# A graph network on one core: the row-index lookups of the second layer move from the relation loop to ahead of the second message stage

## The chip, the cores and the metric

The kernel runs on one core of a Trainium2 chip. The metric is the device time of one execution in microseconds (us), lower is better. Engines are named as in the profile: PE is TensorE (its weight loads stand apart as PEld), DVE is VectorE, ACT is ScalarE, POOL is GpSimd, and SP is SyncE, which here only issues DMAs.

## The reference

Four graph layers on 625 nodes of 768 features and 10,000 edges, each behind a layer norm with relu and added to `x`. What matters here is the first two. Layer L0 is two relational convolutions in a row with 8 relations, layer L1 is one with 34 relations, followed by a graph convolution:

```python
def _rgcn_conv(x, src, dst, etype, W, root, b):        # L0, twice, 8 relations
    seg = dst * num_rel + etype
    sums = segment_sum(x[src], seg); cnt = segment_sum(ones, seg)
    mean = (sums / maximum(cnt, 1)).reshape(num_nodes, num_rel, -1)
    return einsum('nri,rio->no', mean, W) + x @ root + b

# L1: the same with 34 relations, then xw = h1 @ W_gcn and a
# degree-normed sum over the edges
# L2: two attention layers (8 heads, then 1); L3: one with 12 heads
```

## The kernel before

**Tiles.** The nodes are NG = 5 groups of 128. The edges are sorted by destination group in the kernel and stand in NT = 84 tiles of 128 edges. The sum over edges is not taken first, as in the reference, but last: for each relation r the kernel computes `h @ W[r]` for the nodes and stores the rows to an array `U` in HBM; then, edge tile by edge tile, it gathers the 128 rows of `U` that the edges need and adds them to their destinations with a matmul against a weighted one-hot.

**Stages, in the order of the engines' own programs.** Phase C1 (products of the first convolution, 8 relations), messages 0; phase C2 (second convolution), messages 1; layer norm; the relation stage of L1 (34 relations in 17 pairs), messages 2; then the graph convolution and the attention layers. A product step is 18 matmuls of 128x384 (weights and activations are split into a high and a low part, `w_hi`, `w_lo`, `hT_hi`, `hT_lo`; ACT copies the high part, DVE subtracts for the low part, "the split", L848 and L1040). SP loads the weight halves into two buffers `raw` and stores the results.

**Message stages.** `gathers(phase)` on POOL (L472 to L479) issues 84 indirect DMAs from `U`, 384 KB each, into a ring of RB = 8 buffers; before each it waits until PE is done with the tile that had the buffer (`agg_pe`). PE (`messages`, L1471) waits for the one-hot of DVE (L965) and for the gather. The index table of phases 0 and 1 is `ix[:, 0]`; that of phase 2 is `ix[:, 3]`.

**Why L1 needs a lookup.** In L1 most nodes are no source of a given relation, so the products run on compact lists: for each relation the kernel lists its source nodes (at most TC x 128 = 256 in the main part, the rest in "further" tiles), gathers only these rows of `h` and multiplies them. Where the row of node n in relation r stands in `U` is then no longer r x 640 + n; it is in a table `urow`, which DVE computes in `sources` (L968) in phase C2 and signals with `key_ok`. SP stores it to `urow_d` in HBM inside phase C2 (L327 to L330, `urow_st`). POOL looks up, for each of the 84 edge tiles, 128 words of `urow_d` by the indices `ix[:, 1]` (an indirect DMA into one column of `urow_g`) and casts six columns at a time to integers in `ix[:, 3]` (`urow_out`, L505 to L508).

**POOL's program around the change.** The queue is in order. (1) The kinv loop, L483 to L489: 7 rounds of GU = 12 indirect DMAs in two groups of GB = 6, each group behind an index copy (`indices`, L466). (2) `gathers(0)`. (3) Wait for `ov_ok`, which DVE gives in `further_list` (L988 to L1000) after the last relation of phase C2: a scan, two operations of 6,528 elements on one partition (L991, L994) and a few small ones. Then the waits for the stores of C2 and `gathers(1)`. (4) The relation stage: an unrolled list of 17 blocks b. In each, for two relations, POOL waits until PE has turned the old rows (`hc_tp`), and gathers TC = 2 x 128 rows of `h_d` with indices straight from `lidx`. In blocks 0 to 13 six lookups follow, and in 1 to 14 the cast of the block before. (5) The further tiles and `gathers(2)`.

**Beside POOL in phase C2.** After `sources`, DVE transposes the keys (`keys`) and then writes, between the splits, the one-hots of the 34 node lists (`list_one_hot`, L1002, five f16 operations each), with which PE makes `lidx` (L1112).

**The relation stage on the other engines.** PE does per pair 8 product steps, 24 transposes of gathered rows (L1588) and, in pairs 0 to 13, six tiles of edge counts for the graph convolution (L1468), whose one-hots DVE writes two tiles ahead (L918, L954). ACT waits for the weight half (L607) and for PE, copies it, evacuates the products.

## Time and profile before

| | us |
|---|---|
| time, median of 3 runs | 2400.8 (2396.45 to 2413.4) |
| profiled run: device time | 2400.8 |
| profiled run: span of the trace | 2399.0 |
| PE busy | 2065.2 (86%) |
| DVE busy | 1118.9 (47%) |
| ACT busy | 722.4 (30%) |
| POOL busy | 556.2 (23%) |
| DMA, all queues | 378.31 MB, mean 158 GB/s |

All positions in time are microseconds from the start of the span of the profiled run. The busy time of PE is modelled at its ends, since matmuls overlap. "idle before, releaser" is how long the engine stood before an instruction and whose work ended that wait. A row of the order of time reads: start, duration, engine, line of the kernel, operation, what is written from what.

### The profile page before, as it was taken

To read this page: it belongs to the slowest core of one execution; us is meant where nothing else is said; L and a number is where in the kernel's file an instruction comes from. 1 tells how busy PE (TensorE), PEld (TensorE's weight loads), DVE (VectorE), ACT (ScalarE), POOL (GpSimd) and SP (SyncE) were. 2 spreads that over 40 slices of the span, in tenths; PEclk is the share of its full clock that TensorE was granted. 3 is DMA by queue.
4 is the path that set the end of the run, shared out by engine and by line. 5 is a ranking of instruction groups with operands and counts; after the bars stand their busy time and mean duration, and the time that the engine had idled before them with its cause. 6 is when DMAs were issued, how large, how long until landed. Compare 5 with 4: busy or idle time off the path is not lost.

```text
span 2399.0 us, 33918 instructions
## 1 busy us (share of the span) xinstructions
PE 2065.2 (86%) x10740; PEld 1728.6 (72%) x10741; DVE 1118.9 (47%) x2046; ACT 722.4 (30%) x944; POOL 556.2 (23%) x538
## 2 busy tenths in 40 slices
PE   3999789989999999689999999967989768767885
PEld 3999787558789985389989999964556746647663
DVE  5752122234343652435555555532233776656773
ACT  1222121012212210035545554531010256312763
POOL 0000765630000046324444453104620000000000
PEclk8999899999999999889999999988999889885998
DMA  3556456844446458548878777857840021110111
GB/s 108 156 157 185 137 152 210 267 151 130 138 148 188 154 175 268 173 130 264 262 255 261 251 259 250 267 194 238 268 156 8 0 68 28 53 31 26 53 50 38
DMA packets 203264, 378.31 MB, mean 158 GB/s; under 512 B 18810, under 2 KB 173626, under 8 KB 203176
## 3 DMA queue, kind: packets, MB, share of 16 engines
q1 hardware_dynamic: 170520, 246.23, 31.7%
q0 software_dynamic: 31216, 128.89, 17.6%
q10 hardware_dynamic: 1440, 1.97, 0.2%
q8 instruction: 62, 1.02, 0.2%
q14 instruction: 26, 0.21, 0.0%
HBM read 288.68 MB, written 88.34 MB: 157 GB/s over the span
## 4 chain that ended last, share of the span: by engine, by line
PE 74%; DVE 10%; issue 6%; DMA 4%; ACT 4%; ACTq 0%; another core or an unknown queue 0%; SPq 0%; DVEq 0%; POOL 0%; POOLq 0%
PE ps L1575 41%; PE ps L1483 14%; PE ps L1773 5%; PE ps L1738 2%; DMA arena<-in_L_gnn_W_rel 2%; PE ps L1588 2%; PE ps L1701 1%; PE ps L1809 1%; ACT arena L731 1%; PE ps L1468 1%; PE ps L1466 1%; PE ps L1824 1%; PE ps L1427 1%; DVE counts L899 1%; DVE arena L1240 1%
## 5 line engine op out<-in xcount | busy, mean ns | idle before, releaser
L1575 PE MATMUL ps<-w_hi,hT_hi 128*128 128x384 f32 x2172 | 766.0, 353 | 62.3 <-issue 25.6
L1575 PE MATMUL ps<-w_hi,hT_lo 128*128 128x384 f32 x2172 | 738.5, 340 | 0.8 <-issue 0.8
L1575 PE MATMUL ps<-w_lo,hT_hi 128*128 128x384 f32 x2172 | 738.3, 340 | 0.0
L1575 PEld LDWEIGHTS ps<-w_hi,hT_hi 128*128 128x128 f32 x2172 | 418.1, 193 | 75.0 <-issue 54.4
L1575 PEld LDWEIGHTS ps<-w_lo,hT_hi 128*128 128x128 f32 x2172 | 418.2, 193 | 0.2
L1575 PEld LDWEIGHTS ps<-w_hi,hT_lo 128*128 128x128 f32 x2172 | 416.7, 192 | 1.0 <-issue 0.9
L478 POOL DMA_INDIRECT arena<-U,ix x252 | 252.6, 1002 | 521.5 <-DVE ov L1000 355.0
L1483 PE MATMUL ps<-arena,onehot 128*128 128x512 f32 x1008 | 336.6, 493 | 32.2 <-issue 19.7
L1483 PEld LDWEIGHTS ps<-arena,onehot 128*128 128x128 f32 x1008 | 189.8, 191 | 179.6 <-issue 167.7
L1040 DVE TENSOR_TENSOR w_lo<-arena,w_hi 128x2304 fp32r<-128x2304 f32 x67 | 171.4, 2558 | 139.0 <-ACT w_hi L609 131.3
L558 ACT ACTIVATE arena<-ps 128x384 f32<-128x384 f32 x160 | 78.3, 491 | 494.5 <-PE ps L1575 449.1
L965 DVE TENSOR_SCALAR onehot<-iota,tab,wgt 128x128 f32<-128x128 f32 x252 | 82.2, 360 | 270.6 <-PE ps L1483 236.5
L848 DVE TENSOR_TENSOR w_lo<-arena,w_hi 128x2304 fp32r<-128x2304 f32 x45 | 114.9, 2555 | 165.4 <-ACT w_hi L551 134.2
L514 POOL DMA_INDIRECT h<-h_d,lidx x68 | 100.6, 1480 | 317.1 <-PE ps L1588 272.6
L609 ACT ACTIVATE w_hi<-arena 128x2304 fp32r<-128x2304 f32 x67 | 142.5, 2127 | 54.7 <-DMA arena<-in_L_gnn_W_rel 48.3
L1773 PE MATMUL ps<-arena,R 128*65 128x320 f32 (+1 forms) x400 | 125.4, 437 | 30.6 <-ACT arena L731 30.5
L614 ACT ACTIVATE arena<-ps 128x384 f32<-128x384 f32 x136 | 66.4, 488 | 203.4 <-PE ps L1575 189.5
L1299 DVE TENSOR_TENSOR arena<-arena,ps 128x640 f32<-128x640 f32 x105 | 85.7, 819 | 75.1 <-PE ps L1738 67.5
L1427 PE MATMUL ps<-ident,h 128*128 128x128 f32 x210 | 43.6, 376 | 85.1 <-DVE h L832 60.5
L1012 DVE SCALAR_TENSOR_TENSOR hT_lo<-ps,hT_hi 128x512 fp32r<-128x512 f32 x102 | 70.0, 686 | 97.6 <-ACT hT_hi L591 71.0
L523 POOL DMA_INDIRECT urow_g<-urow_d,ix x84 | 103.2, 1229 | 23.7 <-issue 22.0
L1773 PEld LDWEIGHTS ps<-arena,R 128*65 128x65 f32 (+1 forms) x400 | 55.6, 147 | 65.7 <-ACT arena L731 23.4
(238 smaller groups left out, 2179.4 us busy)
## 6 DMA issues: line engine op xcount, KB each, us to landing
arena<-in_L_gnn_W_rel SPq DMA_DIRECT2D x74, 1152.0 KB, 5.6
U<-arena SPq DMA_DIRECT2D x292, 192.0 KB
arena<-in_L_gnn_W SPq DMA_DIRECT2D x36, 1152.0 KB
U<-z SPq DMA_DIRECT2D x28, 864.0 KB
arena<-rows_d SPq DMA_DIRECT2D x42, 320.0 KB, 3.4
arena<-in_L_gnn_root SPq DMA_DIRECT2D x4, 1152.0 KB
arena<-U,ix POOLq DMA_INDIRECT x252
arena<-in_L_gnn_W_root SPq DMA_DIRECT2D x2, 1152.0 KB
```

The source lines that it names most:

```text
L478: pool.indirect_dma_start(out=ring[:, b, :], out_offset=None, in_=U[0:NP * (R0, R0, R1)[phase], :], in_offset=bass.IndirectOffsetOnAxis(ap ...
L514: pool.indirect_dma_start(out=src_rows[:, TC * j + g, :], out_offset=None, in_=h_d, in_offset=bass.IndirectOffsetOnAxis(ap=lidx[:, 2 * TC ...
L523: pool.indirect_dma_start(out=urow_g[:, GB * (b % 2) + k:GB * (b % 2) + k + 1], out_offset=None, in_=urow_d, in_offset=bass.IndirectOffset ...
L558: act.activation(dst, ps[:, (o + g) % 2, 0:HALF] if len(dst.shape) == 2 else ps[:, (o + g) % 2, 0:HALF].rearrange("p (h c) -> p h c", h=ds ...
L609: act.activation(w_hi[:, 1 - j], raw[:, 1 - j], cp).then_inc(S["w_hi"], 1)
L848: dve.tensor_tensor(w_lo[:, o % 2], raw[:, o % 2], w_hi[:, o % 2].bitcast(F32), ALU.subtract).then_inc(S["w_lo"], 1)
L965: dve.tensor_scalar(onehot[:, b, :], iota[:, 1:P + 1], tab[:, 1, ds(t, 1)], wgt[:, ph // 2, ds(t, 1)], ALU.is_equal, ALU.mult).then_inc(S[ ...
L1040: dve.tensor_tensor(w_lo[:, 1 - j], raw[:, 1 - j], w_hi[:, 1 - j].bitcast(F32), ALU.subtract).then_inc(S["w_lo"], 1)
L1299: dve.tensor_tensor(z, z, terms(i % 2), ALU.add).then_inc(s["l_ok"], 1)
L1483: ins = pe.matmul(sums(c0, g), onehot[:, b, :], ring[:, n % RB, c0:c1], start=False, stop=True, skip_group_check=True)
L1575: ins = pe.matmul(acc, l, r[:, j, kt, :], start=(n == 0), stop=(n == 3 * KT - 1))
L1773: ins = pe.matmul(ps[0:c + 1, 2 + b, 0:NP // 2], R[:, t, (c + 1) * hd:(c + 1) * (hd + 1)], pt[:, k % 2, NP // 2 * b:NP // 2 * (b + 1)], st ...
```

## The change

Only POOL's program changes, and one small tile is added. The 84 lookups with their 14 casts leave the relation stage. They stand now between `gathers(0)` and the wait for `ov_ok`, behind a wait for `urow_st`, as a loop of 7 rounds with two groups of six; each group is behind an index copy into `ixb` (as in the kinv loop) and each cast comes one group later. The relation stage becomes a loop of 17 rounds; because its position in `lidx` is now a register's value, the two index columns of each half are copied to a small tile `lixb` first, and POOL waits for its own copy (`lix_ok`). What is computed stays the same.

```diff
+        lixb = sb("lixb", [P, 2, TC], I32)
...
             gathers(0)
 
+            pool.wait_ge(S["urow_st"], 16)
+            def urow_out(it, j):
+                pool.wait_ge(k_in[j], 16 * GB * it + 16 * GB * (NT // GU + 1))
+                pool.tensor_copy(ix[:, 3, ds(GU * it + GB * j, GB)], urow_g[:, GB * j:GB * (j + 1)]).then_inc(S["urow_ok"], 1)
+
+            def lookup(it, first):
+                for j in range(2):
+                    indices(1, it, GB * j, 1)
+                    if not (first and j == 0):
+                        pool.wait_ge(S["urow_ok"], 2 * it + j - 1 + 1)
+                        pool.sem_inc(S["pool_nop"], 1)
+                    for k in range(GB * j, GB * (j + 1)):
+                        pool.indirect_dma_start(out=urow_g[:, k:k + 1], out_offset=None, in_=urow_d,
+                                                in_offset=bass.IndirectOffsetOnAxis(ap=ixb[:, k:k + 1], axis=0)).then_inc(k_in[j], 16)
+                    if j == 1:
+                        urow_out(it, 0)
+                    elif not first:
+                        urow_out(it - 1, 1)
+            pool.sem_inc(S["urow_ok"], 1)
+            lookup(0, True)
+            with pool.Fori(1, NT // GU) as it:
+                lookup(it, False)
+            urow_out(NT // GU - 1, 1)
+            pool.wait_ge(S["urow_ok"], NT // GB + 1)
             pool.wait_ge(S["ov_ok"], 1)
...
             gathers(1)
...
-            pool.wait_ge(S["urow_st"], 16)
-            def urow_out(b):
-                pool.wait_ge(k_in[b % 2], 16 * GB * (NT // GU + b // 2 + 1))
-                pool.tensor_copy(ix[:, 3, GB * b:GB * (b + 1)], urow_g[:, GB * (b % 2):GB * (b % 2 + 1)]).then_inc(S["urow_ok"], 1)
-
-            for b in range(R1 // 2):
+            with pool.Fori(0, R1 // 2) as it:
                 for j in range(2):
-                    pool.wait_ge(S["hc_tp"], 6 * b + 3 * j + 3)
+                    pool.wait_ge(S["hc_tp"], 6 * it + 3 * j + 3)
+                    pool.tensor_copy(lixb[:, j, :], lidx[:, ds(2 * TC * it + TC * j, TC)]).then_inc(S["lix_ok"], 1)
+                    pool.wait_ge(S["lix_ok"], 2 * it + j + 1)
+                    pool.sem_inc(S["pool_nop"], 1)
                     for g in range(TC):
                         pool.indirect_dma_start(out=src_rows[:, TC * j + g, :], out_offset=None, in_=h_d,
-                                                in_offset=bass.IndirectOffsetOnAxis(ap=lidx[:, 2 * TC * b + TC * j + g:2 * TC * b + TC * j + g + 1],
-                                                                                    axis=0)).then_inc(hc_in[j], 16)
-                if 0 < b <= NT // GB:
-                    urow_out(b - 1)
-                if b < NT // GB:
-                    if b >= 2:
-                        pool.wait_ge(S["urow_ok"], b - 1)
-                    for k in range(GB):
-                        pool.indirect_dma_start(out=urow_g[:, GB * (b % 2) + k:GB * (b % 2) + k + 1], out_offset=None, in_=urow_d,
-                                                in_offset=bass.IndirectOffsetOnAxis(ap=ix[:, 1, GB * b + k:GB * b + k + 1], axis=0)).then_inc(k_in[b % 2], 16)
-            pool.wait_ge(S["urow_ok"], NT // GB)
+                                                in_offset=bass.IndirectOffsetOnAxis(ap=lixb[:, j, g:g + 1], axis=0)).then_inc(hc_in[j], 16)
```

## Rows read from the trace of the kernel before

**Rows 1.** The page, busy time of each engine and share of the span

```profile
PE 2065.2 (86%) x10740; PEld 1728.6 (72%) x10741; DVE 1118.9 (47%) x2046; ACT 722.4 (30%) x944; POOL 556.2 (23%) x538
```

**Rows 2.** POOL in order of time: start, us, what, [idle before <- releaser]

```profile
865.30 5.09 POOL L478 DMA_INDIRECT arena<-U,ix  x1 [355.00 <-DVE ov L1000]
```

**Rows 3.** SP's issues in order of time, in phase C2

```profile
741.72 0.27 SPq L330 DMA_DIRECT2D urow_d<-counts  x1
```

**Rows 4.** DMA issues of the whole kernel: median us from issue to landing last

```profile
kinv_d<-kinv SPq DMA_DIRECT2D x1, 105.0 KB, 5.1
...
h<-h_d,vidx POOLq DMA_INDIRECT x3, 4.2
```

**Rows 5.** POOL in order of time, the kinv loop

```profile
238.11 0.19 POOL L468 COPY ixb<-ix 128x6 int32 x1 [233.29 <-DMA kinv_d<-kinv]
239.24 1.12 POOL L488 DMA_INDIRECT counts<-kinv_d,ixb  x1 [0.94 <-POOL ixb L468]
...
260.80 2.56 POOL L488 DMA_INDIRECT counts<-kinv_d,ixb  x1 [0.30 <-issue]
...
323.46 2.93 POOL L488 DMA_INDIRECT counts<-kinv_d,ixb  x1 [0.30 <-issue]
...
347.90 0.19 POOL L468 COPY ixb<-ix 128x6 int32 x1 [3.78 <-DVE wgt L944]
...
363.32 0.94 POOL L488 DMA_INDIRECT counts<-kinv_d,ixb  x1 [0.30 <-issue]
```

**Rows 6.** POOL in order of time, the relation stage

```profile
1083.74 0.24 POOL L508 CAST ix<-urow_g 128x6 int32<-128x6 f32 x1
1084.14 0.96 POOL L523 DMA_INDIRECT urow_g<-urow_d,ix  x1 [0.16 <-issue]
...
1122.44 0.94 POOL L523 DMA_INDIRECT urow_g<-urow_d,ix  x1 [0.31 <-issue]
```

**Rows 7.** DVE in order of time, four stretches

```profile
259.99 2.55 DVE L848 TENSOR_TENSOR w_lo<-arena,w_hi 128x2304 fp32r<-128x2304 f32 x1
...
757.77 2.56 DVE L848 TENSOR_TENSOR w_lo<-arena,w_hi 128x2304 fp32r<-128x2304 f32 x1 [12.99 <-ACT w_hi L551]
...
841.10 2.06 DVE L1006 TENSOR_SCALAR h<-iota,keyT 128x256 f16<-128x256 f16 x10 [1.70 <-PE ps L1566]
...
847.16 2.56 DVE L848 TENSOR_TENSOR w_lo<-arena,w_hi 128x2304 fp32r<-128x2304 f32 x1 [1.82 <-ACT w_hi L551]
...
850.02 6.95 DVE L991 TENSOR_TENSOR arena<-counts,iota 1x6528 f16<-1x6528 f32 x1
...
1122.24 0.25 DVE L918 TENSOR_SCALAR oh_d<-iota,tab 128x128 f16<-128x128 f16 x1
```

**Rows 8.** The chain that ended last, in order of time: start, us, what

```profile
880.25 36.57 PE ps L1483 x112
...
999.45 4.23 DVE R L1149 x2
...
1772.30 4.23 DVE h L1149 x2
```

**Rows 9.** POOL and PE in order of time, start of messages 2

```profile
1641.65 0.94 POOL L478 DMA_INDIRECT arena<-U,ix  x1 [21.76 <-DMA U<-arena]
...
1646.84 4.53 PE L1483 MATMUL ps<-arena,onehot 128*128 128x512 f32 x8 [2.24 <-DVE onehot L965]
```

**Rows 10.** Windows: length, busy us (instructions) by engine, clock, DMA share, GB/s

```profile
1004.00:1009.00 5.00, 0.00 (x0) 0.00 (x0) 4.96 (x4) 0.00 (x0) 0.00 (x0) 0.50 0.00 0
...
1479.39:1508.84 29.45, 28.62 (x175) 27.86 (x174) 15.19 (x17) 15.20 (x19) 6.98 (x6) 1.00 0.84 270
1508.84:1537.39 28.55, 27.92 (x170) 27.40 (x169) 13.93 (x11) 15.29 (x19) 6.43 (x4) 1.00 0.83 274
```

**Rows 11.** POOL in order of time, the second block's later half

```profile
1080.39 2.09 POOL L514 DMA_INDIRECT h<-h_d,lidx  x1 [10.26 <-PE ps L1588]
```

**Rows 12.** Waits from 1080 to 1479: us in total, times, longest

```profile
ACT w_hi L609 <- DMA arena<-in_L_gnn_W_rel: 44.4, 24, 3.4
```

2 lines of the change are left out of this document (1 added, 1 removed).

## The prediction

> **What bounds the kernel now.** I read the page first, then POOL's own order of time, then DVE, PE and the DMA queue in the stretches where POOL's work is moved from and to. The page has PE busy for 86% of the span and POOL for 23% [rows 1]: what POOL does costs time only where PE waits for it. There is one such place near the change. POOL stands idle for 355.00 us, and its first message gather of the second convolution goes out at 865.30, right behind DVE's L1000 (`ov_ok`) [rows 2]. That gather takes 5.09 us where an ordinary one takes 0.94 [rows 2, 5]. PE then works through the 84 tiles of this message stage from 880.25 until DVE takes over at 999.45, 119.2 us [rows 8]. Between POOL's first gather and PE's first message matmul lie 15 us, in which the eight-buffer ring fills while PE ends its products. A later POOL uses up that head start first, and PE's time after it.
>
> The other place is the relation stage: 17 pairs of relations, PE nearly always busy (28.62 of 29.45 us in one pair) [rows 10]; 14 of them carry six lookups each.
>
> **Where the lookups go.** The change takes 84 lookups and 14 casts out of the relation pairs and puts them between `gathers(0)` and `gathers(1)`, in front of the wait on `ov_ok`. They can't use the whole 355 us: they need `urow_st`, and SP issues that store only at 741.72 [rows 3]. A store of much the same size, kinv_d, took 5.1 us to land [rows 4], which gives 746.8; there is a block of zeroes and a weight load in the same queue, so I take 747.5, with 746.8 and 750 as ends.
>
> What is then queued behind them on POOL is `gathers(1)`, and behind that PE's messages. Their length, step by step:
>
> 1. The closest thing that ran is the kinv loop, the same 14 groups of one index copy and six gathers. It ran from 238.11 to 363.32 + 0.94 = 364.26, 126.15 us, of which 3.78 were a wait for DVE's `w_done` [rows 5]: 122.37 are left.
> 2. Four of its gathers were long, from 2.56 for the first to 2.93 for the last, with a mean of 2.71 over the four, against 0.94 for an ordinary one: each cost about 1.76. The first lies over a DVE weight split, a TENSOR_TENSOR of 2.55 us that started at 259.99 [rows 5, 7]. I read this as: a two-input DVE operation holds POOL's gather until about 0.8 us past what the gather would have taken (2.56 - 1.76 = 0.80). Without the four: 122.37 - 7.04 = 115.3 us for 84 bare lookups with their copies.
> 3. `urow_out` adds a cast of 0.24 us and a gap of 0.16 before the next lookup [rows 6], 14 times: 5.6 us. Its DMA is one group old, except for the last one, which waits for its own landing: an indirect DMA took 4.2 us from issue to landing [rows 4], less the 0.94 of the issue: 3.3 us.
> 4. That is 747.5 + 115.3 + 5.6 + 3.3 = 871.7, already past 865.30. Now DVE's two-input operations in that time: six weight splits, from 757.77 to 847.16 [rows 7], 6 x 1.76 = 10.6; L991, a TENSOR_TENSOR of 6.95 us on one partition at 850.02 [rows 7], 6.95 - 0.80 = 6.1 if one partition holds POOL as 128 do, and 0 if not; and the split with the bias add behind it that DVE runs right after `ov_ok`, which cost the gather of 865.30 its 5.09 - 0.94 = 4.1 [rows 2] and will cost the same to a lookup. Together 20.8, so the lookups end and `gathers(1)` begins at **892.5**, 27.2 us later than now. I take the 6.1: the row it is nearest to is the other TENSOR_TENSORs.
>
> The Trainium skill (Advanced Engine Details and Errata, GPSIMD Details) says that the pool engine conflicts with DVE instructions that have two SBUF inputs. The trace agrees with it in the splits [rows 5, 7]; the rule names no number of partitions, so by it L991 counts too, which is the sum above; if one partition were too little to hold POOL, the start would be 886.4. No row so far has POOL at work beside an operation on one partition.
>
> **What the delay costs.** The third message stage shows what a start without a filled ring is worth: POOL's first gather at 1641.65, PE's first message matmul at 1646.84, DVE's take-over at 1772.30 [rows 8, 9]. That is 130.65 us from first gather to the end, and it holds a cold TensorE as well: PE stood idle before it, as it did in 1004 to 1009, where the granted clock was 0.50, the 1.2 GHz level [rows 10]. Here PE starts its messages at 892.5 + (1646.84 - 1641.65) = 897.7 instead of 880.25 and idles in between, so the same holds. End of the stage: 892.5 + 130.65 = 1023.1 against 999.45, **+23.7 us**. The low end is PE starting at 897.7 and keeping today's 119.2 us, and L991 costing nothing: 1016.9 - 6.1 = 1010.8, +11.3. The high end is a store that lands at 750: +26.2. All that follows (layer norm, the relation stage) starts behind this stage and moves with it.
>
> In their new place the lookups also share the time with phase C2's weight loads and PE's products. I cost that at nothing: PE's products set the pace there and the loads come a half phase ahead. DVE's splits were 2.55 us beside a streaming POOL and 2.56 beside an idle one [rows 7], so DVE isn't held by POOL.
>
> **What the relation stage gains.** POOL issues six gathers and a cast fewer per pair, and instead copies two index columns and waits for its own copy before each half: 0.19 + 0.94 us by the kinv loop's copy and the issue at 239.24 [rows 5]. That delays the rows of `h_d` by 1.1 us. A half's rows are gathered as soon as PE has turned the old ones and are turned themselves about 19 us later (half a pair and one product step); an indirect DMA lands in 4.2 [rows 4]. So I cost it at nothing; without this room it would be 34 x 1.1 = 37 us. PE gains only if the lookups disturbed something. From 1080.39 to 1479.39 [rows 10, 11] 13 pairs took 399.0 us, 30.69 each; the next pair, whose PE work is the same and which has no lookups, took 29.45, and the one after, with neither lookups nor counts, 28.55 [rows 10]. ACT waited 44.4 us for relation weights in the 13 pairs [rows 12], so the DMA queue does set the pace in places. The bounds are 0 and 14 x (30.69 - 29.45) = 17.4 us. The pair of 29.45 had also lost part of DVE's one-hots for the counts, which run two tiles ahead, so not all of its 1.24 belongs to the lookups; I take about half, **-8 us**. The changed loop (`Fori` for an unrolled list) I cost at nothing, as a gather of the kinv `Fori` took 0.94 [rows 5].
>
> **Sum.** 23.7 - 8 = +15.7 us. The span of the profiled run is 2399.0, its time 2400.8, which is also the median: 2400.8 + 15.7 = **2416.5 us**. By the bounds of the terms: 2400.8 + 11.3 - 17.4 = 2394.7 to 2400.8 + 26.2 = 2427.0.
>
> **Rivals.**
> - *The f16 lists lock POOL out as well.* Ahead of 843 DVE writes the node lists' one-hots in runs of f16 operations, 14 of them of 2.06 us; the last is at 841.10 [rows 7]. If a run holds POOL as a split does, this is 14 x (2.06 - 0.80) = 17.6 us more: 2434.1. Against it: the lookup of 1122.44 took 0.94 with an f16 TENSOR_SCALAR of 1122.24 beside it [rows 6, 7]. For it: that was one operation, not ten. The Trainium skill (SBUF — State Buffer, Who interferes with whom) has GpSimd unable to write descriptors while DVE is in a 2-port perf mode, which such a one-input operation may be in; the row beside it doesn't show that.
> - *The ring streams.* Today POOL waits for PE once in some eight tiles and PE for a moment with it: 119.2 us for 84 tiles, while the first 28 tiles took 36.57 us, 1.31 each [rows 8]. A POOL that is never held by a full ring could feed PE at that rate: 84 x 1.31 = 109.7, end at 1007.4, +8.0, total 2400.8. Against it: the third stage started this way and took longer, not shorter [rows 8, 9].
> - *The other side: the relation weights come early again.* If the lookups are what makes the loads late, a pair can fall to the 28.55 of the one without counts: 14 x 2.14 = 30 us, and the total is 2400.8 + 23.7 - 30 = 2394.5, not slower. It decides from 23.7 / 14 = 1.7 us a pair. For it: ACT's 44.4 / 13 = 3.4 us a pair [rows 12]. Against it: the counts' own PE work is in that difference.
> - *The lookups are hidden in full.* It would need them to end by 865.3, so to start near 720, and the store is issued at 741.72 [rows 3]. I give it next to nothing.
>
> **How the numbers follow.** Forecast (2405 to 2427) 0.57, f16 lock 0.12, streaming ring 0.15, early weights 0.10, the rest 0.06. A difference under 1%, 24 us, is about what can't be told from no change here. Slower by more is the f16 rival and the top of the forecast, 0.12 + 0.08 = 0.20; faster by more, under 2377, needs the early weights and no delay at once, 0.03; within it 0.77. The range 2392 to 2432 takes in the bounds, the two mild rivals and some 5 us over the top, and leaves out the f16 case and little else.
>
> **What would show it.** In the changed profile: the lookups between 747 and 893, with long ones at the splits and one of about 7 us at 850; the first gather of the second message stage near 892 at 0.95 us; PE idle with a falling clock from 879 to 898; the stage's end near 1023; pairs of 30.1 us in the relation stage. The forecast is wrong if the lookups end by 875, if PE's message stage takes 110 us, or if the pairs drop under 29 or stay at 30.7.

## The result, and the profile after

| | kernel before | changed kernel |
|---|---|---|
| median, run beside each other | 2407.1 us (2396.45 to 2423.96) | 2470.0 us (2464.44 to 2480.22) |
| ratio | | 1.0271, 95% interval 1.0234 to 1.0308 |
| span of the profiled execution | 2399.0 us | 2483.4 us |
| mean granted clock of TensorE | 0.937 | 0.918 |

The changed kernel is slower by 2.7%, some 65 us, four times what I had forecast. Its profiled execution lies 15 us above its own median, so I compare positions inside the traces rather than the spans' ends. I call the message stages first, second and third; the expectations below count them from 0, as in messages 0, 1 and 2, so that their "message stage 1" is the second. Lines of `kernel.py` behind the changed block have moved by 12 (L1000 is now L1012).

First GpSimd (POOL) in order of time, the answer to [rows 2]. Columns: start and length in us, engine, line, operation, and in brackets how long the engine had been idle and what ended it.

```profile
752.32 0.19 POOL L469 COPY ixb<-ix 128x6 int32<-128x6 int32 x1 [237.52 <-DMA urow_d<-counts]
...
754.57 0.95 POOL L509 DMA_INDIRECT urow_g<-urow_d,ixb  x1 [0.30 <-issue]
...
849.94 2.72 POOL L509 DMA_INDIRECT urow_g<-urow_d,ixb  x1 [0.94 <-issue]
...
878.98 0.21 POOL L500 CAST ix<-urow_g 128x6 int32<-128x6 f32 x1 [2.72 <-DMA urow_g<-urow_d,ixb]
...
939.25 4.59 POOL L479 DMA_INDIRECT arena<-U,ix  x1 [60.05 <-DVE ov L1012]
```

The lookups were done at 879.2, earlier than I had put them. POOL then stood idle for 60 us, again behind VectorE's `ov_ok`, and the first gather of the second message stage went out at 939.25, not at 865.30 [rows 2]: 73.95 us later. Of these, 4.5 us were there before any lookup, since SP issued the store of `urow` at 746.19, for 741.72 before [rows 3]. Executions differ in this where their programs don't: in twelve other traces, with the same program up to that point, the store is issued between 733.6 and 741.2.

```profile
746.19 0.27 SPq L331 DMA_DIRECT2D urow_d<-counts  x1
```

Counted from that store, `ov_ok` came after 192.1 us instead of 123.2, 69.0 us late. So it isn't POOL that is late, it is what leads to `ov_ok`, phase C2 itself. The chain of work that ended last shows that this delay is about the whole loss of the medians. Before, VectorE took over from the second message stage at 999.45 and from the third at 1772.30 [rows 8]:

```profile
1072.52 4.23 DVE R L1161 x2
...
1849.26 4.23 DVE h L1161 x2
```

Those are 73.1 and 77.0 us later, 68.6 and 72.5 counted from the store. The second message stage has kept its length, and the stretch between the two marks is 3.9 us longer in this trace. Next come busy times in three stretches (us in each: TensorE matmuls, weight loads, VectorE, ScalarE, POOL; then TensorE's granted clock, the DMA engines' busy share, GB/s). Before the change:

```profile
744.00:865.00 121.00, 121.00 (x978) 117.51 (x977) 66.89 (x192) 31.43 (x42) 0.00 (x0) 1.00 0.52 164
```

After it:

```profile
744.00:755.00 11.00, 11.00 (x66) 11.00 (x65) 2.56 (x1) 4.04 (x5) 1.58 (x3) 1.00 0.79 229
755.00:880.00 125.00, 80.19 (x467) 70.08 (x467) 26.83 (x94) 15.59 (x21) 88.57 (x110) 0.71 0.27 80
880.00:953.00 73.00, 71.69 (x548) 68.61 (x548) 47.05 (x102) 16.71 (x24) 11.62 (x8) 0.98 0.45 145
```

While the lookups run, TensorE (PE) is idle for 44.8 of 125 us and its granted clock falls to a mean of 0.71; before them and after them it is as busy as ever. The DMA engines are at 0.27, less than before, so it is no shortage of bandwidth. The waits in that stretch (engine, line, what ended the wait: us in total, times, longest) are, before the change:

```profile
ACT arena L558 <- PE ps L1575: 77.3, 29, 3.3
DVE h L1006 <- PE ps L1566: 25.4, 15, 2.4
```

and after it:

```profile
ACT arena L570 <- remote: 68.0, 7, 17.7
DVE h L1018 <- remote: 59.5, 7, 20.3
...
PE ps L1578 <- issue: 24.8, 19, 4.2
...
DVE keyT L995 <- remote: 16.1, 1, 16.1
```

"remote" is what the profile writes when it finds nobody who released the wait at that time. Before the change there is no such wait in the stretch at all. ScalarE (ACT) and VectorE (DVE) wait up to 20 us for something that, by the trace, nobody did at that time, and PE's own matmuls come late for no wait at all ("issue"). What that is, and what brings it about, is what the experiments ask.

### The profile page after: what moved, and what is told of

Its sections match the earlier page's. It is cut to its first block, busy times and chain, and to the rows that moved or that the text cites. A ratio compares the mean times of both kernels' runs of the same rounds, so it can differ in the third digit from the quotient of the medians.

```text
span 2483.4 us, 34231 instructions
## 1 busy us (share of the span) xinstructions
PE 2102.0 (85%) x10740; PEld 1753.5 (71%) x10741; DVE 1119.7 (45%) x2046; ACT 723.5 (29%) x944; POOL 561.1 (23%) x586
## 4 chain that ended last, share of the span: by engine, by line
PE 70%; DVE 10%; issue 7%; DMA 5%; ACT 4%; another core or an unknown queue 3%; ACTq 0%; SPq 0%; DVEq 0%; POOL 0%; POOLq 0%
PE ps L1587 38%; PE ps L1495 13%; PE ps L1785 4%; PE ps L1750 2%; DMA arena<-in_L_gnn_W_rel 2%; PE ps L1600 1%; PE ps L1713 1%; PE ps L1821 1%; ACT arena L743 1%; PE ps L1480 1%; PE ps L1439 1%; PE ps L1836 1%; PE ps L1478 1%; DVE counts L911 1%
## 5 line engine op out<-in xcount | busy, mean ns | idle before, releaser
L1587 PE MATMUL ps<-w_hi,hT_hi 128*128 128x384 f32 x2172 | 775.6, 357 | 70.6 <-issue 28.4
L1587 PE MATMUL ps<-w_lo,hT_hi 128*128 128x384 f32 x2172 | 748.5, 345 | 3.7 <-issue 3.7
L1587 PE MATMUL ps<-w_hi,hT_lo 128*128 128x384 f32 x2172 | 747.4, 344 | 3.5 <-issue 3.4
L1587 PEld LDWEIGHTS ps<-w_hi,hT_hi 128*128 128x128 f32 x2172 | 425.4, 196 | 85.1 <-issue 55.0
L1587 PEld LDWEIGHTS ps<-w_lo,hT_hi 128*128 128x128 f32 x2172 | 424.7, 196 | 8.1 <-issue 7.9
L1587 PEld LDWEIGHTS ps<-w_hi,hT_lo 128*128 128x128 f32 x2172 | 423.7, 195 | 4.5 <-issue 4.4
L621 ACT ACTIVATE w_hi<-arena 128x2304 fp32r<-128x2304 f32 x67 | 142.6, 2129 | 59.0 <-DMA arena<-in_L_gnn_W_rel 58.8
L532 POOL COPY lixb<-lidx 128x2 int32 x34 | 30.7, 902 | 391.0 <-PE ps L1600 357.9
L469 POOL COPY ixb<-ix 128x6 int32 (+1 forms) x28 | 5.6, 198 | 480.1 <-DMA urow_d<-counts 237.5
L1439 PEld LDWEIGHTS ps<-ident,h 128*128 128x128 f32 x210 | 36.9, 206 | 93.5 <-DVE h L844 32.1
```

The lines of the kernel that those rows point to most:

```text
L621: act.activation(w_hi[:, 1 - j], raw[:, 1 - j], cp).then_inc(S["w_hi"], 1)
L1439: ins = pe.transpose(psf[:, 512 * b + P * g:512 * b + P * (g + 1)], h[:, g, P * kt:P * (kt + 1)], ident[:])
L1587: ins = pe.matmul(acc, l, r[:, j, kt, :], start=(n == 0), stop=(n == 3 * KT - 1))
```

## The experiments

Unless a text says otherwise, each is an edit of the kernel before, with 72 more lookups whose results nobody uses ("extra lookups"). They are the changed kernel's own code with a target of its own:

```diff
             gathers(0)
+            pool.wait_ge(S["urow_st"], 16)
+            # as urow_out / lookup of the changed kernel, but into dum_g, dum_i; 12 a round
+            more(0, True)
+            with pool.Fori(1, 6) as it:
+                more(it, False)
+            ...
             pool.wait_ge(S["ov_ok"], 1)
```

With 72 of them they end in time for `ov_ok`, so that their own end holds nothing up. I began with theory A: the engines run unrolled code for the first time in this stretch, and the lookups starve their instruction supply.

### Is it the lookups, and does the relation stage gain?

`e1_none` is the changed kernel without its lookups. It leaves the last index table a copy of the first, so that the third message stage gathers as many rows as before, but the wrong ones:

```diff
-            lookup(0, True)
-            ...
+            pool.tensor_copy(ix[:, 3, :], ix[:, 0, :]).then_inc(S["urow_ok"], 1)
```

> The changed kernel without the 84 lookups: GpSimd fills the last index table with a copy of the first one, so message stage 2 gathers the wrong rows, as many and as large as before; all else of the change stays (the loop, the index copies, the wait). Theory A (all that was lost comes from the lookups in their new place): the gathers of message stage 1 begin at 865 us again, the relation pairs stay at 30.5 us each because the lookups were never what held them, and the time is that of the kernel before, 2395 to 2412 us, ratio 0.995 to 1.005. Rival B (the loop form or the index copies of the relation stage cost something themselves): 2415 us or more even without a lookup. Rival C (the lookups did cost the relation stage of the kernel before what I forecast, 8 us): 2399 us with pairs of 29.9 us.

Measured: 2397.2 us beside 2393.7, ratio 1.0015 (0.9995 to 1.0035). The first gather of the second message stage stands at 863.2. What was lost comes from the lookups; the loop and the index copies of the relation stage cost nothing that can be measured. What the relation stage gains is seen on its 67 weight splits on VectorE (first and last start in us); before, in the changed kernel, and without lookups:

```profile
L1040 DVE TENSOR_TENSOR w_lo<-arena,w_hi x67: 2537/2558/2598, 1070.2 to 1570.5; 128x2304 fp32r<-128x2304 f32 x67
```

```profile
L1052 DVE TENSOR_TENSOR w_lo<-arena,w_hi x67: 2539/2559/2560, 1144.1 to 1646.0; 128x2304 fp32r<-128x2304 f32 x67
```

```profile
L1030 DVE TENSOR_TENSOR w_lo<-arena,w_hi x67: 2540/2559/2586, 1064.7 to 1572.6; 128x2304 fp32r<-128x2304 f32 x67
```

500.3, 501.9 and 507.9 us: no gain without the lookups. Single traces of this stage differ by more than the 8 us in question, so I also took the stretch between the two take-overs of [rows 8] from more of them. It is 770.1 to 777.1 us in the four traces without lookups in the relation stage (`after`, `e1_none`, `e1_peloop`, `e4_after_gap`; mean 774.2) and 768.8 to 778.7 us in ten traces with them (mean 774.4). ACT's waits for the relation weights are 48.3 us over the stage before, 58.8 after, 62.1 without any lookup, so the lookups were not what made the weights late. Rival C finds no support.

### The same lookups without the rest of the change

`e1_d4_lists` is the edit shown above.

> The kernel before with 72 more lookups of 4 bytes a row, the same instructions that the change moves, from the same table, between gathers(0) and the wait for ov_ok; their result is used by nobody and the 84 real lookups stay in the relation stage. They should end near 858 us, so they cannot hold the gathers of message stage 1 by their own end. Theory A (they starve the engines that run straight-line instructions beside them): ov_ok comes some 50 to 60 us late, the total is 2450 to 2465 us, ratio 1.021 to 1.027, with TensorE at under 5 us busy in ten and its waits ended by issue. Rival D (the late start of the gathers, as in my forecast, is what costs, and the rest is something else in the change): no more than 5 us, 2402 to 2408 us.

Measured: 2442.8 us, ratio 1.0199 (1.0165 to 1.0234), a little under the expected range: 48 us for 72 lookups. The second message stage begins at 906.1 with POOL idle for 51.9 us ahead of it; `ov_ok` is 46.6 us late, counted from the store of `urow`. The lookups alone do it, without making POOL late. Rival D, my forecast's own mechanism, isn't the loss.

### Beside the loops instead of the unrolled lists

`e1_d4_loops` begins them as soon as `gathers(0)` are issued, `e2_d4_resident`, with 60 lookups, only when the loops of phase C2 are in their second round. Both read single words of `kinv_d`, because `urow_d` isn't there yet:

```diff
-            pool.wait_ge(S["urow_st"], 16)
+            pool.wait_ge(S["c_pe"], 28)        # e2_d4_resident; no wait at all in e1_d4_loops
```

> The same 72 extra lookups, from the table kinv_d read as single words, begun as soon as gathers(0) are issued at about 510 us and done by about 620, where TensorE, VectorE, ScalarE and SyncE all go round their loops of phase C2 (same weights, same stores, same splits as later in the phase). Theory A (straight-line instructions are starved, loops are not): no loss, 2398 to 2410 us, ratio within 0.995 to 1.005. Rival E (the small packets stand in the way of the weights and stores) and rival F (GpSimd and VectorE hold each other up at the memory port): the same loss as among the lists, 2440 us or more.

> 60 extra lookups of 4 bytes (table kinv_d as single words, five rounds of twelve, back to back) that start only when 26 count tiles are done, so near 607 us, and end near 700 us. The run with the extra lookups from 510 us on lost its time between 507 and 612 us, which is the way into phase C2 (written straight) and the first round of the loops; here everything beside the lookups is the second to fourth round of the same loops, whose instructions have been fetched before. Theory A (only instructions that are fetched anew are late): no loss, ratio 0.996 to 1.005, and TensorE at 9.5 to 10 us busy in ten between 610 and 700. Rival E (small packets against weights and stores), rival F (memory port of GpSimd and VectorE) and rival G (any dense stretch of lookups slows whatever runs): about five sixths of the loss of the early one, 35 to 50 us, ratio 1.015 to 1.02.

Measured: 1.0206 (1.0151 to 1.0262) and 1.0173 (1.0126 to 1.0221). Both lose as much for each lookup as the one among the lists (0.68 and 0.69 us against 0.66). Theory A is wrong: the loss doesn't need unrolled code. In the second run the engines go round loops that they have been through before. The Trainium skill (Runtime: NRT & Kernel Launch, Instruction fetch mechanics) says that engines fetch instructions by a DMA queue of their own; in this trace that queue isn't among those that moved anything between 620 and 700 us, while TensorE was busy for 50.33 of the 80 us. This is the queue table of that stretch (packets, MB, share), and TensorE's windows around it:

```profile
q1 hardware_dynamic: 4642, 5.93, 22.7%
q0 software_dynamic: 1568, 0.03, 1.5%
```

```profile
610.00:620.00 10.00, 10.00 (x57) 8.15 (x57) 2.12 (x10) 0.49 (x1) 7.29 (x11) 1.00 0.16 53
620.00:700.00 80.00, 50.33 (x206) 37.43 (x205) 17.03 (x55) 8.98 (x12) 50.27 (x65) 0.77 0.24 74
700.00:710.00 10.00, 10.00 (x57) 8.15 (x57) 3.34 (x16) 3.05 (x3) 0.00 (x0) 1.00 0.23 77
```

### PE's lists as a loop

`e1_peloop` is the changed kernel, made for theory A:

```diff
-                    for it in range(lo, nr):
+                    with pe.Fori(0, nr - lo) as it:
                         for i in range(2 * NG):
-                            step(it, o + i // NG, i % NG)
+                            step(it, o + 2 * lo + i // NG, i % NG)
```

> The changed kernel with the two half phases of TensorE's node-list part made one loop body that runs twice, the order of its products and lists unchanged (list 17 waits for one list more). Theory A: the second round of the body is not fed anew, so about half of the lists are issued at full pace; TensorE's loss between 760 and 880 us falls by a third to a half, the total by 20 to 35 us, to 2435 to 2450 us. If what is starved is VectorE's or SyncE's straight-line part: no change. Rivals E and F: no change, 2465 to 2475 us.

Measured: 1.0226 (1.0177 to 1.0275), against 1.0271 (1.0234 to 1.0308) for the changed kernel. The intervals overlap. The time itself, 2449.2 us, lies inside theory A's 2435 to 2450, but the kernel before ran 13 us faster beside it than beside the changed kernel, and by the ratios only 11 us lie between the two, less than theory A asked for. Both rounds of the loop body are disturbed in the trace. Beside the run before it this decides nothing for A.

### Packets or bytes

`e2_d4_16p` runs each lookup on 16 partitions instead of 128, `e2_d168_lists` fetches 168 bytes a row instead of 4:

```diff
-  indirect_dma_start(out=dum_g[:, k, :], in_=urow_d, in_offset=...(ap=ixb[:, k:k + 1], ...))
+  indirect_dma_start(out=dum_g[0:16, k, :], in_=urow_d, in_offset=...(ap=ixb[0:16, k:k + 1], ...))
+  indirect_dma_start(out=dum_g[:, k, :], in_=kinv_d, in_offset=...)   # the other kernel, 42 words a row
```

> The 72 extra lookups at the node lists, each for 16 partitions instead of 128: the same number of instructions on GpSimd, an eighth of the rows and of the packets. If the packets hold up the instruction fetches: a loss of an eighth, 4 to 12 us, ratio 1.002 to 1.005. If what holds them up is the issue itself (one fixed cost of about 1 us per lookup on GpSimd and what it writes for it): the loss stays near 49 us, ratio 1.018 or more.

> The 72 extra lookups at the node lists with rows of 168 bytes (table kinv_d) instead of 4 bytes: as many packets, 42 times the bytes. If the number of packets is what counts: the same loss as with 4 bytes, 44 to 54 us, ratio 1.018 to 1.023. If bytes count: more, ratio over 1.03. If it is something special to elements of 4 bytes: less than 20 us.

Measured: 1.0227 (1.0196 to 1.0258) with 42 times the bytes, not to be told from the 4-byte rows. With an eighth of the rows 1.0332 (1.0306 to 1.0358): 80 us, far worse than with all of them. So it isn't bytes or rows. On packets the run says nothing, other than I had expected: the queue table (740 to 860 us) has 2304 packets for the 72 lookups on 128 partitions and as many on 16, 32 for each lookup, and also 2304 with rows of 168 bytes.

```profile
q0 software_dynamic: 2304, 0.04, 1.4%
```

```profile
q0 software_dynamic: 2304, 0.01, 1.0%
```

The trace with 16 partitions shows most clearly what goes wrong. PE in order of time, then ACT:

```profile
775.20 0.34 PE L1608 MATMUL ps<-w_hi,hT_lo 128*128 128x384 f32 x1
...
801.50 0.48 PE L1608 MATMUL ps<-w_hi,hT_lo 128*128 128x384 f32 x1 [2.32 <-issue]
839.85 0.69 PE L1608 MATMUL ps<-w_hi,hT_hi 128*128 128x384 f32 x1 [37.87 <-issue]
```

```profile
789.61 0.49 ACT L591 ACTIVATE arena<-ps 128x384 f32<-128x384 f32 x1 [19.31 <-remote]
839.31 0.49 ACT L591 ACTIVATE arena<-ps 128x384 f32<-128x384 f32 x1 [49.21 <-remote]
```

```profile
800.00:840.00 40.00, 0.63 (x2) 0.44 (x2) 0.00 (x0) 0.49 (x1) 25.31 (x39) 0.50 0.01 0
```

Products go to two banks in turn, and PE may start one when ACT has copied out the one before the last. One product ended at 775.54, the next at 801.98. ACT, which has nothing else to do from 790.10 on, copies the first of them out only at 839.31, 64 us after its end, and PE, which waits for that bank, goes on half a microsecond later. The product of 801.98 is copied out at 848.65, after 47 us. Between 800 and 840 PE, DVE, ACT and the DMA engines all stand nearly still; only POOL goes on issuing lookups, one every 1.14 us. The queue table of these 40 us has one row, the lookups' own. By it no instructions were fetched, so theory A fails here too, and no store was under way for which ACT could have waited:

```profile
q0 software_dynamic: 896, 0.00, 1.1%
```

### The gap between two lookups

So I looked at what is different in POOL's own rows: with 128 partitions a lookup follows the one before it after 1.25 us, with 16 after 1.14. In `e2_d4_paced` each is issued when the one before has landed; in `e3_gap05`, `e3_gap1` and `e4_gap01` POOL runs a small memset between two; `e3_half` has 36 lookups with no gap; `e3_pool_busy` has memsets only.

```diff
                             pool.indirect_dma_start(out=dum_g[...], ...).then_inc(dk[j], 16)
+                            pool.wait_ge(dk[0], 16 * GB * it + 16 * k + 16)            # e2_d4_paced, 30 lookups
+                            pool.memset(arena[:, 10000:10512], 0.0).then_inc(fill, 1)  # e3_gap05, 48 lookups
```

(`e3_gap1`: 1072 words and 36 lookups; `e4_gap01`: 128 words and 72 lookups.)

> The extra lookups at the node lists again, but 30 instead of 72, each issued only when the one before it has landed, so one every 3.5 to 4 us and spread over the same 110 us. Theory A with the packets as the cause: the loss goes by the number of lookups, 30/72 of 49 us, about 20 us, ratio 1.006 to 1.012. If the loss goes by the time during which lookups are about at all: as with 72, 45 us or more. If there is a threshold (a fetch gets through in each gap): under 6 us.

> The extra lookups at the node lists, 48 of them, with a small memset (512 words a partition, about 0.5 us) on GpSimd behind each, so that one is issued about every 2 us instead of every 1.45. Theory H (as the runs so far leave it: not the instruction fetches, not the packets, but GpSimd's issue of one indirect DMA right behind the other keeps the other engines from their semaphores and their next instructions, and a gap lets them through): under half of what 48 back to back would cost (48/72 of 49 us is 33 us), so 0 to 15 us, ratio below 1.006. If the gap does nothing and each lookup has its price of 0.68 us: 33 us, ratio 1.013. If only a wait for the landing helps (no second lookup under way): also 33 us.

> 36 extra lookups at the node lists with a memset of 1072 words (about 1.05 us) behind each, one every 2.5 us, over the same stretch of 90 us. Theory H: nothing left to measure, 0 to 5 us, ratio within 1.002, TensorE at 10.00 of ten in the node lists as in the run that waited for each landing. Price per lookup: 36/72 of 49, 24 us, ratio 1.010.

> 72 extra lookups at the node lists in the kernel before with a memset of only 128 words a partition (about 0.2 us, the size of the issue gap that is there anyway) behind each. If it is the instruction between two lookups that lets the others through: under 10 us of loss. If it is free time of about half a microsecond: the pace stays near 1.3 us and the loss near that of the 72 without memsets, 35 to 50 us.

> 36 extra lookups at the node lists, back to back, from 747 to about 800 us, with the rest of the stretch to 865 us free of them. Theory H and a price per lookup both say about half of the loss of 72: 20 to 28 us, ratio 1.008 to 1.012; this is the run to hold against the 36 spaced ones. If the stretch behind the lookups has slack that takes the loss in again: under 10 us.

> No extra lookup at all: in their place 144 memsets of 900 words a partition, one after the other, which keep GpSimd busy about as long (130 to 160 us from 747 us, so the gathers of message stage 1 begin up to 40 us late for that reason alone, which costs at most as much). Theory H: the way to ov_ok is not disturbed, TensorE 10.00 of ten and ov_ok at 864 us. If GpSimd's work on the on-chip memory slows VectorE (rival F): ov_ok late by 10 us or more and VectorE's splits longer than 2.56 us.

Measured, with the runs above. The pace is the usual time from one lookup to the next within a group of six, where VectorE holds none; the loss is (ratio - 1) times the median of the kernel before beside it:

| kernel | pace, us | lookups | ratio (95%) | loss, us | for each lookup |
|---|---|---|---|---|---|
| e2_d4_16p | 1.14 | 72 | 1.0332 (1.0306 to 1.0358) | 79.7 | 1.11 |
| e2_d168_lists | 1.25 | 72 | 1.0227 (1.0196 to 1.0258) | 54.5 | 0.76 |
| e1_d4_lists | 1.25 | 72 | 1.0199 (1.0165 to 1.0234) | 47.6 | 0.66 |
| e3_half | 1.25 | 36 | 1.0060 (1.0038 to 1.0083) | 14.4 | 0.40 |
| e4_gap01 | 1.34 | 72 | 1.0059 (1.0036 to 1.0083) | 14.1 | 0.20 |
| e3_gap05 | 1.66 | 48 | 1.0001 (0.9987 to 1.0016) | 0 | 0 |
| e3_gap1 | 2.13 | 36 | 1.0068 (1.0044 to 1.0092) | 16.3 | see below |
| e3_pool_busy | none | 0 | 1.0082 (1.0055 to 1.0108) | 19.6 | see below |
| e2_d4_paced | 3 | 30 | 1.0104 (1.0058 to 1.0149) | 25.0 | see below |

With 128 words between two lookups the pace is longer by 0.09 us and two thirds of the loss are gone, with 512 words and 1.66 us all of it. The 0.09 us understate the change: over the whole run of 72 a lookup takes 1.77 us on the mean instead of 1.48 in `e1_d4_lists`, in part because VectorE held six of them (2.1 to 6.9 us) and not three. The loss of `e4_gap01` lies between its two expectations, and 44 us of "remote" waits are left in its phase C2. POOL's rows with the memset of 512 words (`e3_gap05`), and the waits from 744 to 865 us, of which none is "remote" any more:

```profile
799.78 0.54 POOL L516 MEMSET arena<- 128x512 f32 x1
800.48 1.02 POOL L512 DMA_INDIRECT dum_g<-urow_d,ixb  x1 [0.17 <-POOL arena L516]
```

```profile
ACT arena L594 <- PE ps L1611: 59.6, 22, 4.1
...
DVE h L1042 <- PE ps L1602: 15.2, 12, 2.1
```

`e3_half` lost 30% of what 72 lose, less than the half that I expected, so the price of a lookup isn't constant either: it grows with the length of the dense stretch, or it is lower beside the first part of it, where PE has few lists yet; the runs don't tell which. The same is seen inside `e1_d4_lists`: PE is idle for 5.9 of 53 us beside the first 36 lookups and for 23.0 of 55 beside the other 36. In `e2_d4_paced` phase C2 isn't disturbed (`ov_ok` at 864.1, no "remote" wait); what it lost is the late start of the gathers, which the part on the prediction uses.

`e3_gap1` and `e3_pool_busy` missed their expectation for another reason. Neither has a "remote" wait. But DVE is busy for 10.00 us in ten in most of the node lists, with longer operations, and `ov_ok` is 15 and 20 us late, counted from the store of `urow`. In `e3_pool_busy` the memsets themselves then hold the first gather for another 7 us (884.58). The lists' one-hots between 780 and 830 us (busy time and mean ns of one) before, with memsets of 512 words, with 1072, and with memsets of 900 words and no lookup:

```profile
L1006 DVE TENSOR_SCALAR h<-iota,keyT 128x256 f16<-128x256 f16 x113 | 23.5, 282 | 19.5 <-PE ps L1566 19.5
```

```profile
L1042 DVE TENSOR_SCALAR h<-iota,keyT 128x256 f16<-128x256 f16 x113 | 31.8, 456 | 11.5 <-PE ps L1602 11.5
```

```profile
L1042 DVE TENSOR_SCALAR h<-iota,keyT 128x256 f16<-128x256 f16 x92 | 44.0, 848 | 1.8 <-PE ps L1602 1.8
```

```profile
L1022 DVE TENSOR_SCALAR h<-iota,keyT 128x256 f16<-128x256 f16 x94 | 46.6, 912 | 1.4 <-PE ps L1582 1.4
```

An f16 operation of 282 ns now takes nearly as long as the memset beside it (848 ns beside 1011, 912 beside 851), as if each waited for one. With 512 words DVE still has 11.5 us to spare and nothing is lost. The lookups themselves do not do this (the same line in the changed kernel: a mean of 300 ns).

### In the changed kernel itself

`e4_after_gap` puts the memset of 512 words behind each of the 84 lookups of the changed kernel:

```diff
                         pool.indirect_dma_start(out=urow_g[...], ...).then_inc(k_in[j], 16)
+                        ...
+                        pool.memset(arena[:, 10000:10512], 0.0).then_inc(S["bd_z"], 1)
```

> The changed kernel with a memset of 512 words a partition (0.56 us) behind each of its 84 lookups, which then are issued every 1.66 us instead of every 1.25. Theory H (lookups back to back make the other engines late; a GpSimd instruction between them lifts it): the node lists run undisturbed, ov_ok near 864 us (938 in the changed kernel), the lookups end later, near 915 us, and the gathers of message stage 1 start 50 us later than in the kernel before instead of 74; by the price of a late start that the paced run showed (24.5 us for 29.4 us) the total is 2430 to 2448 us, ratio 1.014 to 1.021, below the changed kernel although its lookups take longer. Rival (it is the number of lookups that costs, and the 48 spaced ones happened to lie in slack): ratio 1.027 or more.

Measured: 2455.0 us beside 2393.2, ratio 1.0246 (1.0204 to 1.0288), 7 us above the range, and by its interval not to be told from the changed kernel's 1.0271. The trace answers the question all the same. The waits of its phase C2, then POOL's rows, then TensorE's window before the gathers:

```profile
ACT arena L573 <- PE ps L1590: 62.6, 23, 4.1
...
DVE h L1021 <- PE ps L1581: 14.7, 12, 2.1
```

```profile
917.68 0.95 POOL L509 DMA_INDIRECT urow_g<-urow_d,ixb  x1 [0.17 <-POOL arena L513]
...
921.89 0.97 POOL L479 DMA_INDIRECT arena<-U,ix  x1 [0.81 <-POOL ix L500]
```

```profile
890.00:900.00 10.00, 0.00 (x0) 0.00 (x0) 0.00 (x0) 0.00 (x0) 8.37 (x14) 0.50 0.01 0
```

`ov_ok` came 124.1 us after the store of `urow`, where it was 192.1 in the changed kernel and 123.2 before: with spaced lookups phase C2 runs as before. Now the length of the lookups themselves is what holds the gathers (921.89, 56.6 us late; 64.0 counted from the store, which this trace has 7.4 us early), and all engines wait for POOL. Two ways of losing have been exchanged for each other. It is shown that the number of the 84 lookups isn't what made C2 late, but that they followed each other closely with nothing between them.

### The same lateness in the kernel before

The kernel before issues 84 lookups of its own at this pace, the kinv loop. Its PE is busy for 100.7 of 126 us there (240 to 366), and its own trace has "remote" waits (238 to 370 us):

```profile
ACT arena L558 <- remote: 28.0, 7, 9.2
```

Four kernels try to win that back: `e4_kinv_512` and `e4_kinv_128` put a memset behind each, `e5_kinv_u0` and `e5_kinv_u128` write the loop out, with indices straight from the table, the latter with memsets of 128 words.

```diff
-            with pool.Fori(0, NT // GU) as it:
-                for j in range(GU):
-                    ...
-                        indices(2, it, j, 0)
+            for t in range(NT):
+                if t % GB == 0:
+                    pool.wait_ge(S["w_done"], t // GB + 1)
+                pool.indirect_dma_start(out=kgat[:, t % GU, :], ..., ap=ix[:, 2, t:t + 1], ...)
+                pool.memset(arena[:, 10000:10128], 0.0).then_inc(S["bd_z"], 1)   # u128 only
```

> The kernel before with the memset of 512 words behind each lookup of its first loop (the 84 of 168 bytes, 238 to 366 us), beside which TensorE is idle for 26 us in the kernel before. Theory H: those losses go, TensorE is at 10.00 of ten there, but the loop takes 84 times 1.66 us plus what lies between its batches, about 20 us longer, and VectorE weighs the results between its splits, so part of the gain is given back: 2385 to 2400 us, ratio 0.995 to 1.002. If the idle time there has another cause: the loop's 20 us are added, ratio 1.004 or more.

> The same with 128 words (about 0.2 us) behind each lookup of the first loop. If any instruction between two lookups lets the others through: 2375 to 2388 us, ratio 0.990 to 0.997, better than both kernels. If half a microsecond is needed: no change, 2392 to 2402 us.

> The kernel before with its first lookup loop written out: 84 lookups that take their index straight from the table, without the copy of six indices and its wait before each batch (0.7 us per batch, 14 batches), no memset. The pace is then 1.25 us throughout, the lookups end 10 us earlier (near 356 us instead of 366), but they are denser. Theory H: the other engines are as late as before or later beside them, so that at most a few us are won, 2388 to 2398 us, ratio 0.998 to 1.003. If the lateness does not go by density: 10 us won, ratio 0.995 to 0.997.

> The same loop written out, with the memset of 128 words (0.2 us) behind each lookup: a pace of 1.34 us, end near 354 to 360 us. With the memsets in the loop form TensorE was done with its products of this part by 357 us but waited until 372 us for the last lookups and VectorE's weighing behind them; both then end 10 us sooner. Theory H: 10 to 15 us less than in the loop form with memsets, 2380 to 2392 us, ratio 0.993 to 0.999, better than both kernels. If the lateness is not lifted by a pace of 1.34 us: ratio 1.000 or more.

Measured: 1.0123 (1.0077 to 1.0169), 1.0022 (1.0003 to 1.0041), 1.0116 (1.0092 to 1.0141) and 1.0035 (1.0015 to 1.0056). None beats the kernel before, and each lies above the range of theory H (spacing frees the other engines). With the memset of 128 words in the loop ("remote" waits of ACT down to 11.1 us) PE was done with its products by 355 us but then waited 21.2 us for a split that VectorE did behind its weighing of the last lookups, and the first message stage began no earlier. Written out and with the same memsets, ACT's "remote" waits grew instead (238 to 370 us):

```profile
ACT arena L560 <- remote: 51.8, 9, 14.4
```

So 128 words between two lookups don't lift the lateness by themselves. What the written-out loop without memsets does is the more telling: it only takes away the index copies, the pause of 0.7 us after every sixth lookup. The kernel before and then `e5_kinv_u0`, 250 to 290 us:

```profile
250.00:290.00 40.00, 25.98 (x123) 24.71 (x122) 8.61 (x14) 5.96 (x9) 29.87 (x31) 0.83 0.48 130
```

```profile
250.00:290.00 40.00, 8.15 (x31) 7.48 (x30) 5.13 (x10) 1.29 (x3) 27.33 (x27) 0.61 0.29 69
290.00:300.00 10.00, 10.00 (x51) 10.00 (x52) 0.00 (x0) 2.87 (x4) 0.00 (x0) 0.86 0.24 84
```

Thirty-six lookups without a pause (238.47 to 285.26) leave PE busy for 8.15 of the 40 us, and as soon as POOL stops and waits for VectorE's weighing, PE is at 10.00 of 10. Writing out a loop "to save its overhead" cost 28 us.

## Why the prediction was wrong

I go through it by its own steps.

- **Where the lookups go, and how long they take.** Start: 752.3 for 747.5, of which 4.5 us are the later issue of the store in this execution; from issue to first index copy it took 6.1 us, and I had 5.8. End: 879.2 for 892.5. The lookups and casts took 126.9 us and not 145.0. Most of these 18 us are the long lookups, 20.8 us in my sum and some 5.3 in the trace: I counted six behind splits, one behind L991 and one behind the bias, and there were three (2.53 at 765.37, 2.89 at 786.37, 2.72 at 849.94), because VectorE itself was late and most of those operations came after the lookups. The mechanism was right: in `e4_after_gap`, where VectorE is on time, the one-partition operation of 6.95 us holds a lookup for 6.52 us. The prediction had no such row. It ends 0.8 us after the VectorE operation, as I had reckoned from the splits:

```profile
844.49 6.52 POOL L509 DMA_INDIRECT urow_g<-urow_d,ixb  x1 [0.16 <-POOL arena L513]
```

```profile
843.24 6.95 DVE L1006 TENSOR_TENSOR arena<-counts,iota 1x6528 f16<-1x6528 f32 x1
```

- **What the delay costs.** Right, but it never came to bear. `e2_d4_paced` is the case that I had described: phase C2 undisturbed, lookups up to the gathers, first gather at 893.16 (892.5 forecast for the changed kernel), first message matmul at 897.39 (897.7 forecast). VectorE then takes over from the message stage at 1021.04, 21.6 us later than before; I had 23.7. The total is 25.0 us longer (14 to 36 by its interval).

```profile
893.16 0.96 POOL L482 DMA_INDIRECT arena<-U,ix  x1 [1.24 <-issue]
```

```profile
897.39 23.85 PE L1506 MATMUL ps<-arena,onehot 128*128 128x512 f32 x64 [19.39 <-DMA arena<-U,ix]
```

```profile
1021.04 4.23 DVE R L1172 x2
```

- **"In their new place the lookups also share the time with phase C2's weight loads and PE's products. I cost that at nothing."** This is the step that failed. It held 44.8 us of idle PE and a granted clock of 0.71, and made `ov_ok` 69.0 us late (192.1 us behind the store of `urow` instead of 123.2). My reasons for nothing were that PE's products set the pace, that the weight loads come early, and that DVE's splits take 2.55 us beside a streaming POOL as beside an idle one. The last is true in the changed kernel as well (2.54 to 2.56 us), and it doesn't matter: the splits weren't longer, they began late. The evidence was in the trace of the kernel before. Beside the kinv loop, whose gathers [rows 5] I used as the model for the lookups' length, PE waited on "issue" for 22.2 us and ACT on "remote" for 28.0. I read from that loop what POOL needs and not what the others lose beside it.
- **What the relation stage gains.** I took 8 us of at most 17.4; no gain is seen (500.3 and 501.9 us between the same splits, and the means of 774.4 and 774.2 us above). The pair of 29.45 us without lookups had lost its part of the counts' one-hots, which I had seen and weighed at half. The runs leave nothing of it for the lookups. The six lookups of a pair also never disturbed the stage: no "remote" wait stands in it. They come in bursts of six with some 20 us behind each, in which POOL issues only four gathers of `h`.
- **The rivals.** The f16 lists don't lock POOL (lookups in the changed kernel take 0.95 us beside them). Whether the ring streams, the changed kernel doesn't test: its gathers started 14.5 us ahead of PE, as before, and the message stage took 118.8 us (953.70 to 1072.52) for 119.2. `e2_d4_paced` does: from 897.39 to 1021.04 are 123.7 us, and streaming would have taken 109.7. The relation weights didn't come early. No rival of mine put the loss in phase C2, so the range had nothing there to reach to.

**What stays open.** It is shown that lookups issued one behind the other every 1.14 to 1.34 us make PE, ACT and DVE late (and SP: a register instruction at L307 took up to 0.72 us beside the lookups of the changed kernel, and at most 0.05 in the same stretch before), and that a GpSimd memset of half a microsecond between two lifts it. It isn't shown by what path. Bytes and instruction fetches are excluded, and so are memsets on GpSimd alone, which left no "remote" wait. The number of packets as such is excluded by `e4_after_gap`, which has all 84 lookups; their rate isn't, since each lookup moved 32 packets in the three forms counted. Nor is what GpSimd writes when it issues a DMA. That POOL keeps something occupied which the others need to see a semaphore or to go on in their program is a guess that would fit.

The pace of single pairs isn't the whole condition either. In the second message stage of the kernel before, gathers of 384 KB go out some seven or eight in a row, mostly 1.24 to 1.32 us apart, with a pause of 1.9 to 3.9 us behind them. PE is busy for 111 of 120 us there, and there is one "remote" wait, of 1.8 us:

```profile
880.00:1000.00 120.00, 111.16 (x336) 62.76 (x336) 27.43 (x85) 0.00 (x0) 72.47 (x76) 1.00 0.78 255
```

Pauses between bursts seem to matter as well as the pace within them. Only `e5_kinv_u0` takes them away at an unchanged pace, and ACT's "remote" waits beside the kinv loop (238 to 370 us) then rise from 28.0 to 71.0 us. That the run with 16 partitions is worst because of its shorter pace is argued from the table: no run held the pace fixed and changed the partitions. Nor does any run tell whether the time between two lookups counts or that an instruction stands there: every spaced run with a memset has both.

## What to carry to other kernels

Don't cost a GpSimd queue of back-to-back indirect DMAs at nothing because GpSimd and the DMA engines are idle: look in a trace at what the other engines do beside such a run, and at waits that end on nobody while the producer has long finished. Spread them in bursts of a few with time between them, as the relation stage had, and keep them away from the stretch that sets the pace. Half a microsecond of other GpSimd work behind each frees the other engines too, but the longer queue can cost as much (`e4_after_gap`, `e4_kinv_512`). Work that looks like it is in the way of a long stage may be where it costs least: an idle engine is no proof that its neighbours are free.

## What the runs showed of the hardware that I had not expected

- 72 indirect DMAs at a pace of 1.25 us cost 48 us beside a TensorE-bound stretch, at 1.34 us 14 us, and 48 at 1.66 us nothing. On 16 partitions (pace 1.14 us) they cost 80 us, more than on 128.
- A finished TensorE product was copied out by an idle ScalarE 64 us later (775.54 to 839.31), beside lookups at a pace of 1.14 us.
- An indirect DMA for 16 partitions moved as many packets as one for 128 (32), and took 0.84 us on GpSimd instead of 0.94.
- GpSimd memsets hold up an f16 TENSOR_SCALAR of VectorE: a mean of 282 ns became 848 beside memsets of 1.01 us, and 912 beside memsets of 0.85 us issued without a pause. Indirect DMAs left it at 300.
- A VectorE operation with two inputs on a single partition holds up a GpSimd indirect DMA as one on 128 partitions does (6.52 us beside 6.95).
